# Latent attention with the first third turned in its own slot, and grouped feed-forward with the fold one step sooner

## The reference, cut to what matters

```python
scores = einsum('bqhrd,bkhd->bhrqk', q, k) * scale      # causal
probs = softmax(where(causal, scores, min), axis=-1)
y = einsum('bhrqk,bkhd->bqhrd', probs, v).reshape(Bq, Tq, N_HEADS * HEAD_DIM)
return y @ wo
```

```python
h1 = einsum('gmh,goh->gmo', xg, W1) + b1[:, None, :]
h2 = einsum('gmo,gho->gmh', h1, W2) + b2[:, None, :]
```

## Time and profile before

| | us |
|---|---|
| median of 3 runs | 2833.56 (2832.0 to 2837.6) |
| the profiled execution | 2835.26 |
| its span, first to last instruction | 2833.5 |
| TensorE busy in the span | 2590.6 (91%) |
| VectorE | 2148.7 (76%) |
| ScalarE | 1946.9 (69%) |
| GpSimd | 1114.5 (39%) |

### The profile page before, as it was taken

The page is one execution under the profiler, slowest core; times in us unless marked ns, Lnnn a source line. Parts: engine busy times, 40 slices in busy tenths (PEclk is TensorE's granted clock), DMA queues, the critical chain, the costliest instruction groups (busy, mean ns, idle before and its releaser), DMA issues. The chain is left out here.

```text
span 2833.5 us, 61506 instructions
## 1 busy us (share of the span) xinstructions
PE 2590.6 (91%) x21708; PEld 1733.8 (61%) x21708; DVE 2148.7 (76%) x3970; ACT 1946.9 (69%) x5552; POOL 1114.5 (39%) x1268
## 2 busy tenths in 40 slices
PE   6699898997889989779899999998999999999898
PEld 3476896764654434345567777776446777777643
DVE  4577564776776779767689999996448999999676
ACT  4477565776754544364389999997448999999744
POOL 0244343430004634330065556553216555555431
PEclk9799998997999999889999999999999999999999
DMA  4200120000000000030000000000000000000000
GB/s 150 79 24 24 53 72 28 24 25 8 9 17 1 1 0 1 23 72 1 29 2 2 2 2 2 2 2 21 1 9 2 2 2 2 2 2 2 2 26 34
DMA packets 83168, 53.89 MB, mean 19 GB/s; under 512 B 28848, under 2 KB 75568, under 8 KB 82864
## 3 DMA queue, kind: packets, MB, share of 16 engines
q1 hardware_dynamic: 78768, 41.56, 5.2%
q0 software_dynamic: 4096, 8.40, 1.0%
HBM read 31.59 MB, written 18.35 MB: 18 GB/s over the span
## 5 line engine op out<-in xcount | busy, mean ns | idle before, releaser
L2319 ACT ACTIVATE probs<-banks,minus_max,rnorm 128x128 f32<-128x128 f32 x1024 | 460.1, 469 | 4.3 <-DVE minus_max L2415 4.3
L2222 POOL TENSOR_TENSOR qk_cross<-qk_raw,rope_scaled 128x512 f32<-128x512 f32 x256 | 326.1, 1275 | 12.9 <-ACT qk_raw L2352 0.3
L2188 PE MATMUL banks<-weights,hf 128*128 128x512 f32 x512 | 278.0, 626 | 5.0 <-ACT kt L2348 5.0
L2232 POOL TENSOR_TENSOR qk_rot<-qk_rot,rnorm 128x512 f32<-128x512 f32 x128 | 133.5, 1043 | 285.7 <-DVE qk_rot L2448 285.3
L2319 ACT ACTIVATION_READ_ACCUMULATOR probs<-banks,minus_max,rnorm 128x1 f32 x1024 | 223.2, 218 | 0.0
L2395 DVE COPY probs_t<-banks 128x512 f32<-128x512 f32 x256 | 175.7, 686 | 46.0 <-PE banks L2154 45.4
L2154 PEld LDWEIGHTS banks<-ident,probs 128*128 128x128 f32 x1024 | 126.8, 140 | 136.7 <-issue 132.9
L730 ACT ACTIVATE probs<-banks,minus_max 128x128 f32<-128x128 f32 (+1 forms) x512 | 206.6, 438 | 5.2 <-DVE minus_max L758 5.0
L2441 DVE TENSOR_TENSOR qk_rot<-qk_raw,rope_scaled 128x512 f32<-128x512 f32 x256 | 175.2, 724 | 0.0
L2197 PE MATMUL banks<-ident,qk_rot 128*128 128x128 f32 x1024 | 159.7, 279 | 13.6 <-DVE qk_rot L2448 8.5
L758 DVE TENSOR_REDUCE minus_max<-banks 128x2 f32<-128x256 f32 (+1 forms) x256 | 124.8, 549 | 62.3 <-PE banks L582 62.3
(11 more groups left out here) (368 smaller groups left out, 6929.9 us busy)
## 6 DMA issues: line engine op xcount, KB each, us to landing
sorted_x<-zero_rows SPq DMA_DIRECT2D x10, 512.0 KB, 6.6
rows_in<-sorted_x SPq DMA_DIRECT2D x18, 256.0 KB, 3.1
sorted_y<-rows_out SPq DMA_DIRECT2D x18, 256.0 KB, 2.4
x_res<-in_x SPq DMA_DIRECT2D x8, 512.0 KB, 6.4
out_x<-x_res SPq DMA_DIRECT2D x16, 256.0 KB, 2.0
w1b<-in_L_ffn_w SPq DMA_DIRECT2D x8, 256.0 KB, 4.0
s_branch<-in_L_ffn_w SPq DMA_DIRECT2D x8, 256.0 KB, 5.7
w1g<-in_L_ffn_W SPq DMA_DIRECT2D x8, 256.0 KB, 2.8
```

The lines of the kernel that those rows point to most:

```text
L2188: pe.matmul(ps[:, misc(k, j)], hf[:, n // 2 % 2, 0, n % 2 * P:(n % 2 + 1) * P], wqkv[:, w:w + QW], start=True, stop=True).then_inc(*S[name ...
L2222: return pool.tensor_tensor(by_half(tw[:, n, at]), by_half(qk[:, n, at])[:, :, ::-1, :], tab[:, n, 2 * w + 1].rearrange("p (a d) -> p a d" ...
L2319: last = act.activation(pr[:, k % 2, head], ps[:, 2 * (k % 2) + par, c * P:(c + 1) * P], ACT.Exp, scale=rn[:, k % 4, head:head + 1], bias= ...
```

## The change

In the attention, the lead third of slot g is turned at the end of TensorE's slot g, behind the projection, and no longer in slot g + 1 behind the scores; it then waits for the first half of the exponentials alone, so that these signal twice a slot. The maxima of heads 0 and 1 are taken one head at a time, each with a signal, and each head's exponentials wait for their own. In the feed-forward the fold of group g + 1 heads the even step c = 2g, all folds use bank 0, and the chunks turned back go to banks 1 and 7 by turns, waiting for ScalarE's copy of two chunks before. VectorE's and ScalarE's orders, SyncE's and GpSimd's stay.

```diff
         def pe_scores(pe, i, g):
-            pe.wait_ge(*S["exps"].at(i, g - 1))
+            pe.wait_ge(*S["exps"].at(i, 2 * (g - 1) + 1))
...
         def pe_turn(pe, i, g, t):
-            if t == 0 and not here(i, g + 1, 4):
-                pe.wait_ge(*S["exps"].at(i, g))
+            if t == 0:
+                pe.wait_ge(*S["exps"].at(i, 2 * g))
+            if t == 1 and not here(i, g + 1, 4):
+                pe.wait_ge(*S["exps"].at(i, 2 * g + 1))
...
                     if here(i, g, 4):
                         pe_scores(pe, i, g)
-                    if here(i, g - 1, 4):
-                        pe_turn(pe, i, g - 1, 0)
...
                         pe_project(pe, i, u + 2, lambda c: wk[:, c].rearrange("p r l -> p (r l)"), "k_ps")
+                    if here(i, g, 4):
+                        pe_turn(pe, i, g, 0)
...
                     for s in range(2):
-                        act.wait_ge(*S["rowmax"].at(i, 2 * g + s))
                         for e in range(2):
+                            act.wait_ge(*S["rowmax"].at(i, 3 * g + (2 if s else e)))
...
-                    last.then_inc(*S["exps"].inc)
+                        last.then_inc(*S["exps"].inc)
...
-                    for qb in range(2):
-                        last = dve.tensor_reduce(nm[:, g % 2, s, qb], ps[:, 2 * s:2 * s + 2, qb * P:P + qb * T], AX.X,
-                                                 ALU.max, negate=True)
-                    last.then_inc(*S["rowmax"].inc)
+                    for heads in (slice(0, 2),) if s else (slice(0, 1), slice(1, 2)):
+                        for qb in range(2):
+                            last = dve.tensor_reduce(nm[:, g % 2, s, qb, heads],
+                                                     ps[:, 2 * s + heads.start:2 * s + heads.stop, qb * P:P + qb * T],
+                                                     AX.X, ALU.max, negate=True)
+                        last.then_inc(*S["rowmax"].inc)
...
-    PREP_AT, FFN_AT, IN_AT, BACK_AT = 0, 2, 4, 7
+    PREP_AT, FFN_AT, IN_AT, BACK_AT = 0, 2, 4, (1, 7)
...
                 def fold(g):
-                    pe.wait_ge(*S["v1"].at(0, g - 2))
+                    pe.wait_ge(*S["v1"].at(0, g - 1))
                     for c in range(IT):
-                        pe.matmul(ps[:, PREP_AT + u, 0:P], w1[:, u, c], w2[:, u, c], start=(c == 0), stop=(c == IT - 1))
+                        pe.matmul(ps[:, PREP_AT, 0:P], w1[:, u, c], w2[:, u, c], start=(c == 0), stop=(c == IT - 1))
...
-                    if c >= 0 and c % 2 == 1 and c // 2 + 1 < GROUPS:
+                    if c >= 0 and c % 2 == 0 and c // 2 + 1 < GROUPS:
                         fold(c // 2 + 1)
...
-                        pe.wait_ge(*S["normed"].at(0, n - 1))
+                        pe.wait_ge(*S["normed"].at(0, n - 2))
                         for t in range(W):
-                            mm = pe.transpose(ps[:, BACK_AT, t * P:(t + 1) * P], rows[:, n % 2, t], m["ident"][:])
+                            mm = pe.transpose(ps[:, BACK_AT[n % 2], t * P:(t + 1) * P], rows[:, n % 2, t], m["ident"][:])
```

More of the change, by code:

```diff
@@ L641, in pe_v @@
             mm.then_inc(*S["v_ps"].inc)
-        names = dict(copied=2, scores=8, rowmax=8, exps=4, turned=12, lead_sb=4, turned_sb=8, mixed=4, rowsum=2, widened=2, spread=2,
+        names = dict(copied=2, scores=8, rowmax=12, exps=8, turned=12, lead_sb=4, turned_sb=8, mixed=4, rowsum=2, widened=2, spread=2,
                      spread_sb=2, attended=2, q_ps=2, q_sb=2, k_ps=2, k_sb=2, v_ps=2, v_sb=2, o_ps=2, o_sb=2)
@@ L755, in rowmax @@
                     dve.wait_ge(*S["scores"].at(i, 2 * g + s))
-                    dve.wait_ge(*S["exps"].at(i, g - 2))
-                    for qb in range(2):
-                        last = dve.tensor_reduce(nm[:, g % 2, s, qb], ps[:, 2 * s:2 * s + 2, qb * P:P + qb * T], AX.X,
-                                                 ALU.max, negate=True)
-                    last.then_inc(*S["rowmax"].inc)
+                    dve.wait_ge(*S["exps"].at(i, 2 * (g - 2) + 1))
+                    for heads in (slice(0, 2),) if s else (slice(0, 1), slice(1, 2)):
[4 more added lines that the diff above has]
+                        last.then_inc(*S["rowmax"].inc)
                 def turned(i, g, t):
@@ L770, in slot @@
                     if g % 2 == 0 and here(i, u - 1, 2):
-                        dve.wait_ge(*S["exps"].at(i, g - 1))
+                        dve.wait_ge(*S["exps"].at(i, 2 * (g - 1) + 1))
                         dve.wait_ge(*S["widened"].at(i, u - 2))
@@ L1781, in fold @@
                     pe.wait_ge(*S[f"fetched{u}"].at(0, 4 * (g // 2) + 3))
-                    pe.wait_ge(*S["v1"].at(0, g - 2))
+                    pe.wait_ge(*S["v1"].at(0, g - 1))
                     for c in range(IT):
-                        pe.matmul(ps[:, PREP_AT + u, 0:P], w1[:, u, c], w2[:, u, c], start=(c == 0), stop=(c == IT - 1))
+                        pe.matmul(ps[:, PREP_AT, 0:P], w1[:, u, c], w2[:, u, c], start=(c == 0), stop=(c == IT - 1))
                     for c in range(IT):
-                        mm = pe.matmul(ps[:, PREP_AT + u, P:P + 1], w2[:, u, c], b1[:, u, c:c + 1], start=(c == 0),
+                        mm = pe.matmul(ps[:, PREP_AT, P:P + 1], w2[:, u, c], b1[:, u, c:c + 1], start=(c == 0),
                                        stop=(c == IT - 1))
@@ L1826, in _ @@
                         act.wait_ge(*S["copied"].at(0, n))
-                        act.activation(m["xn"][:, tokens(n)], ps[:, BACK_AT], ACT.Copy).then_inc(*S["normed"].inc)
+                        act.activation(m["xn"][:, tokens(n)], ps[:, BACK_AT[n % 2]], ACT.Copy).then_inc(*S["normed"].inc)
                     if 0 <= c - 4 < R:
@@ L1842, in folded @@
                     dve.wait_ge(*S["silu"].at(0, 2 * g - 3))
-                    dve.tensor_tensor(bc[:, u:u + 1], ps[:, PREP_AT + u, P:P + 1], b2[:, u:u + 1], ALU.add)
-                    dve.tensor_copy(wc[:, u], ps[:, PREP_AT + u, 0:P]).then_inc(*S["v1"].inc)
+                    dve.tensor_tensor(bc[:, u:u + 1], ps[:, PREP_AT, P:P + 1], b2[:, u:u + 1], ALU.add)
+                    dve.tensor_copy(wc[:, u], ps[:, PREP_AT, 0:P]).then_inc(*S["v1"].inc)
                 folded(0)
```

## The result

The changed kernel takes 2839.85 us (median of 20 runs, 2835.35 to 2847.74); the kernel before took 2835.13 us in 20 runs beside them. The ratio is 1.0018, 95% interval 1.0012 to 1.0025: about 5 us slower, where 7 us faster was forecast. The time lies outside the range and on the other side of no change.

The account below looks back on a forecast made before the run. Attention was taken as bound by ScalarE's chain, VectorE's 0.20 us behind; feed-forward by VectorE's fold waits. Attention +4.2 and feed-forward -11.5 gave -7.3 us: 2828.0 from the profiled execution, 2826.3 as median; range 2816 to 2835.

Parts of the forecast that it names:

- The grouped feed-forward: Second stage changed: folding one step sooner ends VectorE's waits, eight steps 32.10 to 22.6 us; stage -11.5 us.
- the fill: Feed-forward stretch before the eight steps: fold waits of 5.0 us there, gain between 0 and 5.0, taken as -2.0 us.
- the last weights: Feed-forward, last group's weights: the sooner fold might wait for them, 0 to 2 us, taken as 0.
- rival 2: Feed-forward wait moves to TensorE, busy 27 us in the eight steps at a lower clock: 2832.7 us; chance 0.22.
- No price of its own: Feed-forward banks: TensorE no longer needs ScalarE's copy of the chunk just before; given no separate gain.
- The split: Attention maxima of the first two heads: two more VectorE reductions cost 0.15 us a slot, bounds 0 and 0.32.
- ScalarE leaves the chain: Attention: with the lead third copied after the exponentials, ScalarE's chain takes 5.2 us and no longer bounds the slot.
- The mix to the scores: Attention slot's last link: 0.79 us before, forecast 0.65, as a 0.20 us wait for ScalarE was to go.
- the second chain: Attention, VectorE's chain from maxima through copies and mix to scores: ends 0.20 us before ScalarE's, allowing at most that gain.
- The matmuls between: Attention, TensorE from projection to mix: 0.87 us for the matmul pair, then 0.49 for the four transposes.
- Rival 3: Attention transposes stand on the chain at full length: +0.465 us a slot on average, +29.8 us, kernel 2851.9; chance 0.07.
- Rival 1: The split pays: each attention slot drops the 0.20 us wait, -12.8 us, kernel 2809.3 us; chance 0.10.

Follow-up runs that it names:

- the two edits: Kernel before with only the fold one step sooner: 2825.06 us, 0.9964; kernel before with only the shared fold bank and two turned-back banks: 2830.04 us, 0.9979.

## Why the prediction was wrong

- *The grouped feed-forward* was right: -12.2 us in the traces and -11.6 alone, for -11.5. The eight steps took 22.26 for 22.6, the fill gave 1.8 (34.64 to 32.85) for 2.0, the last weights cost 0.67 within 0 to 2. TensorE did not become the bound (19.07 us busy, not 27), so rival 2 fell. "No price of its own" for the banks was wrong without harm: they give half of the gain alone, by another way to the same waits.
- *The split* was right: 0.13 us a slot (2.08 for 1.95) against 0.15. The 125 ns that the Trainium skill gives there (Perfetto Trace Analysis, "Optimizing Scalar/DVE Operations") would have made it 0.25, by estimate; the traces have 65 ns for each of the two reductions.
- *ScalarE leaves the chain* was right, and so were the links up to the projection: in the even slot the maxima at 1.22, the copy at 3.22 (3.24 forecast), the projection at 3.95 (3.97).
- *The step that failed* is "The mix to the scores took 0.79, 0.20 of it the wait that goes: between 0.59 and 0.79, I take 0.65". It took 0.79 after, in both slots: 0.14 x 64 = 9.0 us, about half of what the sum missed in the steady slots. With it fell the reading "by those 0.20 us alone": the second chain had nothing to allow, as the split alone showed in its even slot.
- *The matmuls between* are the other half, too short by 0.25 us a pair, 8.0 us: projection to transposes took 0.97 and 0.94 for 0.87, transposes to mix 0.53 for 0.49. I had taken the 0.87 from the output's pair with the v matmuls behind it, not from a projection. The odd slot's projection started 0.06 later than forecast: I had put it 0.05 us behind the output's copy, where its own row before has 0.15 (185.17 to 185.32) and the row after 0.14. The even one's started 0.02 sooner. Together 0.26 and 0.31: 5.98 and 5.92 become 6.24 and 6.23.
- *Over a whole call* the slot grew less than in the pair shown: 183.55 / 31 = 5.92 us became 6.22, and 5.95 became 6.21, +0.28 on average, since its first two intervals got shorter (6.60 and 6.35 us in the first call, then 6.19 and 5.86). That and the ends of the calls (+2.7 and -0.7) make some 19.5 of the +19.9.
- *Rival 3* came nearest. It was to decide from +0.27 us a slot on, and the calls show +0.28; its price (+0.465) was too large, since starts follow starts by less than the records, as I had held against it. It had 0.07. *Rival 1* fell: but for the first two of a call, no slot got shorter.

## What to carry to other kernels

A short idle time with a releaser's name, in front of every instance of one instruction, may be the engine's own gap that the semaphore only happens to fill. Look whether it stays where the releaser is long done; until then give it no value as slack. Where two chains round a loop are equally long, work taken off one and put onto the other lengthens the loop, even if none is added: here four transposes had stood in a time in which TensorE would have waited anyway. The cheap cure was an order that cuts a link out of the ring (2816.08 us for 2839.85 here), not smaller pieces of the work in it.

## What the runs showed of the hardware

The weight loads of the scores (32 x 128) start 0.20 us late behind the mix (128 x 32): before with ScalarE's name, after in 62 places with none. In the changed kernel's slot such a gap, of 0.13 to 0.20 us, stands at each of the four changes of the tile (scores to mask, mask to the next 128 x 128 load, transposes to mix, mix to scores), and none above 0.03 us between loads of the same tile unless they wait for a copy; whether the change of tile makes the gap was not tried. At the end of the first attention call the granted clock averaged 0.75 after the change and 0.93 before it, between the two levels of 1.2 and 2.4 GHz, over 20.47 and 17.73 us: TensorE was idle for about half of each stretch. In the feed-forward's eight steps it rose from 0.87 to 1.00 by either of the two edits, without a matmul taken away; before, VectorE's wait for a fold was 3.7 us where the clock was down and 2.06 where it was not.
